# Expert stages of an eight-stage transformer kernel started block by block: layer norm and routing moved beside tiles of other blocks

## The reference

```python
x = x + 0.5 * _L0_ffn_ref(_layernorm(x, axis=-1), ...)
x = x + _L0_attn_ref(_layernorm(x, axis=-1), ...)      # a state space scan
x = x + 0.5 * _L0_ffn_ref(_layernorm(x, axis=-1), ...)
x = x + 0.5 * _L1_ffn_ref(_layernorm(x, axis=-1), ...) # mixture of experts
x = x + _L1_attn_ref(_layernorm(x, axis=-1), ...)      # attention, 8 heads, one K and V
x = x + 0.5 * _L1_ffn_ref(_layernorm(x, axis=-1), ...) # the same experts again
```

```python
logits = x @ gate_w.T                       # 64 experts
scores = jax.nn.sigmoid(logits)
scores_for_choice = scores + gate_bias[None, :]
grp = scores_for_choice.reshape(T, NG, E // NG)        # 8 groups of 8
group_scores = jnp.sum(jax.lax.top_k(grp, 2)[0], axis=-1)
_, gidx = jax.lax.top_k(group_scores, TOPK_GROUP)      # the best 4 groups
...
_, topk_idx = jax.lax.top_k(masked, TOP_K)             # the best 8 experts
topk_w = topk_w / (jnp.sum(topk_w, axis=-1, keepdims=True) + 1e-20) * ROUTED_SCALE
expert_out = jax.vmap(lambda gw_, uw_, dw_: _mlp(x, gw_, uw_, dw_))(Wg, Wu, Wd)
routed = jnp.einsum('eth,te->th', expert_out, rw)
shared = _mlp(x, Sg, Su, Sd)
```

## Time and profile before

| | |
|---|---|
| median of 3 runs | 1801.06 us (1800.49 to 1803.01) |
| the profiled execution's own time | 1803.61 us |
| its span | 1801.8 us |
| mean granted clock of PE | 0.947 of 2.4 GHz |
| PE / PEld busy | 1614.6 us (90%) / 1208.8 us (67%) |
| DVE / ACT / POOL busy | 1234.6 (69%) / 953.1 (53%) / 902.6 us (50%) |
| DMA | 118.72 MB, 66 GB/s over the span |

### The profile page before, as it was taken

The page is one execution under the profiler, slowest core; times in us unless marked ns, Lnnn a source line. Parts: engine busy times, 40 slices in busy tenths (PEclk is TensorE's granted clock), DMA queues, the critical chain, the costliest instruction groups (busy, mean ns, idle before and its releaser), DMA issues.

```text
span 1801.8 us, 25450 instructions
## 1 busy us (share of the span) xinstructions
PE 1614.6 (90%) x6820; PEld 1208.8 (67%) x6820; DVE 1234.6 (69%) x2015; ACT 953.1 (53%) x1864; POOL 902.6 (50%) x786
## 2 busy tenths in 40 slices
PE   5999558877799985999999997999998599999998
PEld 3777323333367763788888885988885488888887
DVE  4555779999945645666666666877775466666666
ACT  3234565444434342565555564877773265655565
POOL 2000147766610023677777773344433277777776
PEclk9999779999989986999999999999997799999999
DMA  2000000000000001676777760000000366767765
GB/s 111 1 0 1 0 0 1 0 0 1 0 8 1 0 35 37 143 154 144 157 147 149 151 138 1 2 0 0 0 1 9 76 152 145 155 146 154 149 149 119
DMA packets 30035, 118.72 MB, mean 66 GB/s; under 512 B 5323, under 2 KB 17059, under 8 KB 18211
## 3 DMA queue, kind: packets, MB, share of 16 engines
q1 hardware_dynamic: 29987, 118.15, 29.8%
HBM read 116.03 MB, written 2.10 MB: 66 GB/s over the span
## 4 chain that ended last, share of the span: by engine, by line
PE 65%; DVE 3%; issue 2%; POOL 2%; ACT 2%; DMA 1%; POOLq 0%; DVEq 0%; SPq 0%; ACTq 0%
PE ps L218 18%; PE ps L220 18%; PE ps L219 18%; PE ps L1270 2%; PE ps L1255 1%; PE ps L1257 1%; PE ps L1256 1%; POOL m_hc L831 1%; PE ps L621 1%; DMA rwb<-rw_rows 1%; PE ps L240 1%; POOL e_lo L226 1%; PE ps L253 1%; PE ps L1258 1%; DMA rw_rows<-rwt 0%
## 5 line engine op out<-in xcount | busy, mean ns | idle before, releaser
L226 POOL TENSOR_TENSOR e_lo<-e_h,e_hi 128x512 fp32r<-128x512 f32 (+1 forms) x368 | 479.0, 1302 | 258.3 <-ACT e_hi L223 251.2
L1138 DVE TENSOR_TENSOR ps<-e_s,ps 128x512 f32<-128x512 f32 x352 | 245.0, 696 | 237.8 <-PE ps L220 179.1
L963 ACT ACTIVATE e_s<-ps 128x512 f32<-128x512 f32 (+1 forms) x368 | 220.2, 598 | 323.6 <-PE ps L220 323.5
L218 PE MATMUL ps<-xn_hi,eh 128*128 128x512 f32 x704 | 280.4, 398 | 22.8 <-DVE ps L1138 22.8
L219 PE MATMUL ps<-xn_lo,eh 128*128 128x512 f32 x704 | 279.1, 396 | 0.0
L220 PE MATMUL ps<-xn_hi,el 128*128 128x512 f32 x704 | 278.1, 395 | 0.0
L1149 DVE TENSOR_TENSOR e_h<-ps,rwb 128x512 f32<-128x512 f32 x352 | 243.3, 691 | 44.9 <-DMA rwb<-rw_rows 21.3
L223 ACT ACTIVATE e_hi<-e_h 128x512 fp32r<-128x512 f32 (+1 forms) x368 | 229.0, 622 | 48.8 <-DVE e_h L1149 25.7
L831 POOL TENSOR_TENSOR m_hc<-m_h,m_c 128x512 f32<-128x512 f32 x128 | 172.8, 1350 | 126.6 <-DVE m_h L787 124.3
L226 POOL TENSOR_TENSOR xn_lo<-ln_c,xn_hi 128x512 fp32r<-128x512 f32 (+1 forms) x24 | 34.2, 1427 | 327.9 <-ACT xn_hi L223 327.8
L621 PE MATMUL ps<-m_hc,const 128*128 128x512 f32 x256 | 149.3, 666 | 48.7 <-POOL m_hc L831 43.7
(11 more groups left out here) (238 smaller groups left out, 3192.5 us busy)
## 6 DMA issues: line engine op xcount, KB each, us to landing
rwb<-rw_rows SPq DMA_DIRECT2D x32, 704.0 KB
rwb<-rw_rows SPq DMA_DIRECT2D x40, 512.0 KB
e_raw<-in_experts SPq DMA_DIRECT2D x88, 192.0 KB, 5.5
rwb<-rw_rows SPq DMA_DIRECT2D x16, 640.0 KB
rwb<-rw_rows SPq DMA_DIRECT2D x24, 384.0 KB
rwb<-rw_rows SPq DMA_DIRECT2D x16, 448.0 KB
rwb<-rw_rows SPq DMA_DIRECT2D x16, 320.0 KB
rwb<-rw_rows SPq DMA_DIRECT2D x40, 128.0 KB
```

The costliest lines, as they stand in the source:

```text
L218: pe.matmul(out, w_hi, x_hi, start=start, stop=False, skip_group_check=True)
L226: return eng.tensor_tensor(lo, full, hi.bitcast(F32), ALU.subtract)
L963: act.activation(e_s[0:rows_, buf, :], ps[0:rows_, 4, :], ACT.Silu).then_inc(S["silu"], 1)
L1138: dve.tensor_tensor(ps[0:rows_, 6 + buf % 2, :], e_s[0:rows_, buf, :], ps[0:rows_, 5, :], ALU.mult).then_inc(S["gated"], 1)
```

## The change

In words, by stage:

- **F2** (`ffn_pe`, `ffn_act` with R set): the logits of blocks 0 to 2 are computed in it, in blocks 1 to 3, and one Sigmoid each at the end of the block. The next block's first gate matmul waits for that Sigmoid, since both use PSUM bank 0. The shared expert's weights are split here, and the first two chunks of expert weights are loaded.
- **E1 and E2**: routing is cut into four, one for each block, of 24 steps over 4 tiles. Its pieces stand between the shared tiles and the first four expert tiles on DVE. Each block's weights go out to memory and come back by DMAs of their own (`moe_first_rows`). The first pair runs its tiles as chunk 0 and 1 of block 0, then of block 1, and so on (`FIRST_TILES`), the last pair in another order (`LAST_TILES`), so that x of blocks 0 to 2 is ready before the last tile. In the first pair the second multiplication takes both its inputs from SBUF (`first_tile`).
- **E1's end**: the norm of attention's blocks 0 and 1 is computed among the last tiles. Attention's weights are split in the last pair but one, in eight parts, and are loaded from memory twice (once at the start as before, once after chunk 9's rows).
- **Attention** starts with K and V of block 0; the norm of blocks 2 and 3 is spread over its first heads. E2's first weights are loaded during it.
- The loops over blocks in F1, F2 and attention are written out; so are the first and the last two pairs of the experts.

The core of the diff:

```diff
-            ffn_pe(pe, F2, LN[2], LN[3])
+            ffn_pe(pe, F2, LN[2], LN[3], E1)
...
+                        if R and i and layer_ == 1 and k == 2:
+                            route_logits(pe, R, N, i - 1, 0)
...
-                    if following is not None and k < HC - 1:
+                    if i + 1 < NB and k < HC - 1:
                         if k == 0:
                             pe.wait_ge(*L("xn_lo", i + 2))
-                        gate(following, k)
+                            if R and i:
+                                pe.wait_ge(*R("scores", i))
+                        gate(i + 1, k)
...
+                if R and i:
+                    route_scores(act, R, i - 1, 0)
...
+        FIRST_TILES = tuple((c, b) for b in range(NB) for c in range(2))
+        LAST_TILES = ((0, 0), (0, 1), (1, 0), (1, 1), (0, 2), (1, 2), (0, 3), (1, 3))
...
+            def first_tile(j):
+                c, b = FIRST_TILES[j]
+                t = in_pair(0, j)
+                dve.wait_ge(*S("up", t + 1))
+                dve.wait_ge(*S("silu", t + 1))
+                dve.wait_ge(*S("h_lo", t - 3))
+                dve.tensor_tensor(e_h[:, j % 4, :], e_s[:, j % 4, :], ps[:, 5, :], ALU.mult).then_inc(S["gated"], 1)
+                dve.wait_ge(*S("gated", t + 1))
+                if c == 0:
+                    dve.wait_ge(*S(f"rw_first{b}", 96))
+                dve.tensor_tensor(e_h[:, j % 4, :], e_h[:, j % 4, :], rwb[:, c, cut(b)], ALU.mult).then_inc(S["weighted"], 1)
...
+            def routings():
+                shared_gate(2)
+                route_pairs(dve, S, 1)
+                shared_gate(3)
+                route_groups(dve, S, 1)
+                route_mask(dve, S, 1)
+                shared_gate(4)
+                route_top(dve, S, 1)
+                route_weights(dve, S, 1)
+                shared_gate(5)
+                route_pairs(dve, S, 2)
+                route_groups(dve, S, 2)
+                shared_gate(6)
+                route_mask(dve, S, 2)
+                route_top(dve, S, 2)
+                shared_gate(7)
+                first_tile(0)
+                route_weights(dve, S, 2)
+                first_tile(1)
+                route_pairs(dve, S, LAST)
+                route_groups(dve, S, LAST)
+                first_tile(2)
+                route_mask(dve, S, LAST)
+                route_top(dve, S, LAST)
+                first_tile(3)
+                route_weights(dve, S, LAST)
+                for j in range(4, PER):
+                    first_tile(j)
...
+            def row_weights(ch):
+                sp.wait_ge(*S("weighted", SHARED + NB * (ch - 1) if ch > 3 else SHARED + PER + ch - 3))
...
+                if N and j == 4:
+                    pe.wait_ge(*S("x_new", 1))
+                    one_mean(pe, N, 0, 0)
+                if N and j == 5:
+                    pe.wait_ge(*S("x_new", 2))
+                    one_mean(pe, N, 1, 1)
+                    one_var(pe, N, 0, 0)
+                if N and j == 6:
+                    one_var(pe, N, 1, 1)
+                    one_spread(pe, N, 0, 0)
+            if N:
+                one_spread(pe, N, 1, 1)
```

More of the change, by code:

```diff
@@ new lines, in route_scores, with route_turn @@
+        def route_scores(act, R, b, bank):
+            act.wait_ge(*R("logits", b + 1))
+            act.activation(r_s[:, b, :, :].rearrange("p t e -> p (t e)"), ps[:, bank, 0:4 * E], ACT.Sigmoid).then_inc(R["scores"], 1)
+        def route_turn(pe, R, b, bank):
+            pe.wait_ge(*R("route", ROUTE_STEPS * (b + 1)))
+            for t in range(4):
+                last = pe.transpose(ps[0:E, bank, t * P:(t + 1) * P], r_t[:, t * E:(t + 1) * E], ident)
+            last.then_inc(R["rw_t"], 1)
@@ new lines, in route_rows, with of_groups @@
+        def route_rows(act, R, b, bank):
+            act.wait_ge(*R("rw_t", b + 1))
+            act.activation(rwt[:, cut(b)], ps[0:E, bank, :], ACT.Identity).then_inc(R["rwt"], 1)
+        NGT = 4 * NG
+        r_k = [r_small[:, k, :] for k in range(4)]
+        r_c8 = r_c[:, :, :].rearrange("p t (g k) -> p (t g) k", k=8)
+        r_t3 = r_t[:, :].rearrange("p (t e) -> p t e", e=E)
+        r_u3 = r_u[:, :].rearrange("p (t e) -> p t e", e=E)
+        def of_groups(tile, lo, n):
+            return tile[:, lo:lo + NGT * n].rearrange("p (g k) -> p g k", k=n)
@@ L478, in ffn_pe, with ffn_act, block_ @@
                 pe.wait_ge(w_split, 4)
-            ffn_blocks(pe, block_)
-        def ffn_act(act, S, N):
-            def block_(i, blk, before, following):
+            for i in range(NB):
+                block_(i)
+        def ffn_act(act, S, N, R):
+            def block_(i):
+                if R and i == 1:
+                    moe_act(act, R)
                 for o in range(HC):
@@ L940, in moe_act, with moe_act_tiles @@
             act.activation(sd_h[:, :, :], sd_raw[:, :, :], ACT.Identity).then_inc(S["small_hi"], 1)
-        def moe_act_tiles(act, S, attention):
-            load_table(act, ACT.Sigmoid)
-            for half in range(2):
-                act.wait_ge(*S("logits", half + 1))
-                act.activation(r_s[:, 8 * half:8 * half + 8, :].rearrange("p t e -> p (t e)"), ps[:, half, :], ACT.Sigmoid)\
-                    .then_inc(S["scores"], 1)
+        def moe_act_tiles(act, S, L, N):
             def gate_up_high(i, c, read):
@@ L980, in moe_act_tiles @@
+                if t == 6:
+                    route_rows(act, S, 1, 7)
+            silu(SHARED, 0, P)
             high(SHARED - 1, 3, I)
-            silu(SHARED, 0, P)
-            for g in range(4):
-                act.wait_ge(*S("rw_t", g + 1))
-                act.activation(rwt[:, cut(g)], ps[0:E, 6 + g % 2, :], ACT.Identity).then_inc(S["rwt"], 1)
             def pair(i, last):
+                first = isinstance(i, int) and i == 0
+                c0_end = FIRST_TILES.index((0, LAST)) + 1 if first else NB
@@ new lines, in moe_dve @@
+            if S is E1:
+                one_block_left()
+            else:
+                four_blocks_left()
+            dve.wait_ge(*S("rwt", NB))
+            with dve.Fori(1, PAIRS - 1) as i:
+                for j in range(PER):
+                    tile(i, j)
+            for j in range(PER):
+                tile(PAIRS - 1, j, LAST_TILES)
+                if j >= 5:
+                    x_new(j - 5)
+                if N and j >= 6:
+                    one_centre(dve, N, j - 6, j - 6)
@@ L1447, in heads @@
             def heads(i, last):
-                blk = bass.ds(i * T, T) if not last else cut(i)
+                blk = cut(i)
                 for h in range(HEADS):
```

819 lines of the change are left out of this document (489 added, 330 removed).

## The result

The changed kernel took 1837.67 us (median of 4 runs, 1833.79 to 1842.40) against 1802.03 for the kernel before on the same chip (4 runs, 1800.49 to 1804.85): a ratio of 1.0192, with a 95% interval of 1.0169 to 1.0216. It is 35.6 us slower; I had forecast 8.2 us slower and a range up to 1827. The profiled execution has a span of 1834.7 us, 32.9 more than that of before.

A forecast was written before the change was run, and what follows sets the result against it. The prediction took DVE's list and a DMA latency at the stage seams as the limit. Its terms, 7.4 - 6.9 - 5.3 + 12.0 + 1.0 = +8.2 us on 1801.1, gave 1809 us, with a range of 1789 to 1827.

The forecast's parts named there:

- F2's stall: In F2's blocks 1 and 2 the next gate waits 1.7 us for a table load and a Sigmoid.
- F2 as a whole: F2 gets longer by two stalls (3.4 us) and the logits matmuls (4.0 us): +7.4 us.
- The list on DVE: At E1's and E2's start, DVE's operations plus waits and POOL: routing ends 65 and 86.5 us after the barriers.
- the contention: In E1's and E2's routing, 17 POOL operations slow DVE steps by 0.6 us each: 10 us per stage.
- rival 1: POOL's operations fall beside gates, both routings end 10 us earlier, -11.8 us in all, 1789 us; chance 0.27.
- rival 3: Full lock: every POOL operation delays DVE by its length, 11 us more per stage, 1832 us; chance 0.08.
- The trip behind the routing: In E1 and E2, from routing's end through memory: tile 6 after 11.7 us, tile 8 7 us later, 18.7 in all.
- With small pieces I put the whole at 7.0: Block 3's weights in E1 and E2: writing to memory and loading rows until tile 6 takes 7.0 us.
- PE's up, down and transposes 2.2: In E1 and E2, PE's work behind block 3's gate, up to the transposed weights, takes 2.2 us.
- now about one [tile], against 7 us: Chunk 2's rows, waiting for chunk 0's buffer after tile 6, have about one tile's time but need 7 us.
- Attention: Barrier to first transposes needs only K, V, Q, square, scores (13.6 us) and one late spread, 14.6 us: -14.5 us.
- E1's end: From PE's last up to the barrier, the norm among the last tiles lengthens the chain by 9.2 us.

The follow-up runs named there:

- zero_low: Changed kernel, but POOL writes zeros instead of the low part for the eight shared and first four expert tiles, reading nothing from SBUF: 1818.24 us, ratio 1.0083.
- after_16: Changed kernel, but each block's weights go to memory as rows 0 to 15 and 16 to 63, not 0 to 2 and 3 to 63: ratio 1.0122.
- early_turn: Changed kernel, but PE transposes block 3's routing weights after tile 1's down instead of tile 2's, and ACT copies them earlier: ratio 1.0155.
- rows_by_block: Changed kernel, but the rows of chunks 2 and 3 are asked for block by block, in 24 small DMAs instead of 6 large ones: ratio 1.0131.
- no_late_norm: Changed kernel, but the norm of blocks 2 and 3 is left out of attention, so it computes something else: ratio 1.0114.
- the old seam: Changed kernel, but attention's norm of all four blocks stands at attention's start as before, none in E1's last tiles: ratio 1.0166.
- best_16: Changed kernel with second-pair rows by block, block 3's transposes after tile 1, attention's norm whole at its start, writes as rows 0-15 and 16-63: ratio 1.0015.
- b_trip16: Kernel before with transposes right behind routing, block 0's weights written and loaded first, writes as rows 0-15 and 16-63: 1783.13 us, ratio 0.9888.

## Why the prediction was wrong

**What held.** F2's stall (1.7 against 1.68 and 1.66), and F2 as a whole: 7.4 against 7.5 in this profile and 5.2 to 7.6 over nine executions of that code, so that the agreement to 0.1 is luck. The list on DVE: the routing's end in E1 (65.0 against 65.5) and in E2 (86.5 against 88.2), the end of E2's first shared gate (29.9 against 29.0), the contention (10 us per stage against 8.0 and 10.7). E1's routing ends so near the forecast because two errors cancel: POOL cost 2 us less than the 10, and the waits for PE and ACT came to 8.4 us where I had 6. (The prices of a block's 24 steps add up to 8.6 us, not 8.75, which changes the list by 0.6.) The prediction stands with neither rival 1 nor rival 3: POOL costs 0.5 to 0.6 us for each of my 17 operations, near my 0.6 and not the 0.3 of the one or the full 1.26 of the other. The waits at tiles 6 and 8 are there, and E2 reaches tile 8 at 112.5, not before 93. By the Trainium skill ("SBUF — State Buffer", section "Who interferes with whom") a DVE instruction with two SBUF inputs contends with a GpSimd instruction that reads SBUF, not with one that only writes it, and the contention is an exclusive lock. The trace agrees where both read: in E1 the five steps that start within 0.2 us of a POOL operation of 1.26 to 1.28 us are 1.02 to 1.06 us longer, those that start later in it 0.13 to 0.96. zero_low agrees that a POOL that only writes leaves DVE alone.

**The trip behind the routing, 18.7 us, was mis-sized by 6.3 in E1 and 5.6 in E2.** Three sentences of the prediction fail. "With small pieces I put the whole at 7.0": from the write's issue to tile 6 it took 9.3 us in both stages, since I had cut the write without asking how it would be carried out. Three rows and 61 rows go one behind the other, and 61 rows on one engine hold back the rows by 2.5 and 2.7 us (after_16). "PE's up, down and transposes 2.2", with the gate and ACT 3.9 until the write: it was 5.2 in E1 and 4.3 in E2. In E1 3.5 us passed ahead of the transposes alone, with PE's matmuls 0.43 us apart (clock 0.50); early_turn won 3.4 and 2.5 us by moving them. The third step was "now about one [tile], against 7 us" for chunk 2's rows: tile 8 came 10.5 and 10.7 us behind tile 6. In E1 the rows are asked for 0.8 us behind tile 6 and are there 9.7 us later, where the two chunks of the earlier trace rows took 7.8; what makes these 1.9 us isn't shown. That wait is the largest single cost at these seams, 6.4 and 4.6 us (rows_by_block). The sum itself has 0.8 us that it doesn't name: 0.7, 2.2, 1.0 and 7.0 are 10.9, not 11.7.

**Attention, -14.5 us forecast and -3.8 measured.** The step that failed is "K, V, Q, square and scores alone, about 13.6, and one late spread". K, V, Q and scores alone are 14.5 (no_late_norm). But what the change defers is not out of the way: means, variances and spreads of blocks 2 and 3 are written ahead of the first transposes, 24 matmuls with 9.1 us of busy time in the rows above. That is 5.7 us in these two executions (2.2 in the one of rows_by_block, see the last section); 2.5 more are lost in the first heads, where DVE and ACT fit in normalise and splits. I listed this norm under the change and put all of it but one late spread at nothing. How large the miss looks hangs on the execution too: in six of this code attention took 254.8 to 258.2 us, and the changed kernel's profile is the longest. A further 2.6 us of attention stay unassigned; the changed kernels with the old seam have 234.2 to 234.3 us in the same place, and the attention of the kernel before took 232.8 to 233.7 in four kernels, so about 1 of it may be the spread of single executions.

**E1's end** cost 11.3, not 9.2, by the chain that the prediction named. Its steps hold up to the square root, which ends 7.3 us behind the last up, as forecast. Then the two spreads took 2.07 us each and not the 1.10 of the earlier trace rows: PE's clock was 0.50 there, and the rows that I had priced them from were taken at 1.00.

**Rival 3** (1832) came closest in time and for the wrong reason: it wanted a full lock. The direction was right, and the range (up to 1827) missed by 11 us. Both large errors were on the side of the gain, in the two steps in which work was moved and I priced only the part that I was looking at.

## What to carry to other kernels

Before a serial step is cut into pieces, list what each piece issues again (here two writes, six row DMAs and four transposes per block) and where the last piece still stands behind other work: the end is set by the last piece's trip. Tile 0 was weighted 27.9 us earlier in E1, and with the trip repaired 2.6 us of that were left at the stage's end (best_16 against b_trip16). What a stage defers into the next one belongs into that stage's sum with all its matmuls. And where a stall ends in a trip through memory, shorten the trip first: 21 us of it were there from the start, between the end of the routing and tile 0, and moving the transposes and shaping the writes gave 1.1% with the old schedule.
